# Turning layer-norm rows by DMA transposes of 16-bit pairs, in a two-layer attention and feed-forward kernel

## The reference

```python
x = x + tanh(g_xattn[0]) * L0_xattn(layernorm(x), ctx, ...)   # norm 0: 32 heads of 128, 8 key/value heads
x = x + tanh(g_ffn[0])   * L0_ffn(layernorm(x), A, B, Wr, br) # norm 1: 8 experts of rank 16, softmax router
x = x + tanh(g_xattn[1]) * L1_xattn(layernorm(x), ctx, ...)   # norm 2: 16 heads of 96, 4 key/value heads
x = x + tanh(g_ffn[1])   * L1_ffn(layernorm(x), ...)          # norm 3: gated feed-forward, width 1792
```

## Time and profile before

| what | value |
|---|---|
| median of three executions | 1203.42 us |
| the profiled execution's own time | 1202.64 us |
| its span in the trace | 1200.8 us |
| mean granted TensorE clock | 0.988 |
| TensorE busy | 1140.5 us (95%) |
| VectorE busy | 854.8 us (71%) |
| ScalarE busy | 826.8 us (69%) |
| GpSimd busy | 342.4 us (29%) |

### The profile page before, as it was taken

The page is one execution under the profiler, slowest core; times in us unless marked ns, Lnnn a source line. Parts: engine busy times, 40 slices in busy tenths (PEclk is TensorE's granted clock), DMA queues, the critical chain, the costliest instruction groups (busy, mean ns, idle before and its releaser), DMA issues.

```text
span 1200.8 us, 22840 instructions
## 1 busy us (share of the span) xinstructions
PE 1140.5 (95%) x7264; PEld 721.9 (60%) x7264; DVE 854.8 (71%) x2086; ACT 826.8 (69%) x2699; POOL 342.4 (29%) x644
## 2 busy tenths in 40 slices
PE   6789999999999999999999978899999999799998
PEld 4445666665666666666666555566776766355555
DVE  4578767776777677677677778898888888843434
ACT  5688878888888888888778745578777766522221
POOL 5444333335633333343333421111211121000000
PEclk9899999999999999999999989999999999999999
DMA  7454555554765546545564433467987585300000
GB/s 244 103 115 106 128 140 99 119 139 83 153 115 127 129 103 127 119 103 127 136 107 119 93 58 88 90 99 161 227 200 155 129 170 126 62 2 1 36 1 35
DMA packets 390871, 134.31 MB, mean 112 GB/s; under 512 B 365536, under 2 KB 375520, under 8 KB 390752
## 3 DMA queue, kind: packets, MB, share of 16 engines
q1 hardware_dynamic: 388848, 129.19, 49.2%
q0 software_dynamic: 1904, 3.67, 1.0%
HBM read 39.21 MB, written 2.10 MB: 34 GB/s over the span
## 4 chain that ended last, share of the span: by engine, by line
PE 80%; DVE 9%; ACT 5%; issue 3%; POOL 3%; DMA 0%; DVEq 0%; POOLq 0%; ACTq 0%
PE bank L477 23%; PE bank L479 22%; PE bank L478 22%; PE bank L686 8%; PE bank L705 4%; ACT probs L862 1%; DVE stats L1052 1%; DVE pieces L1041 1%; POOL rstd L1437 1%; DVE mx L1142 1%; PE bank L506 1%; ACT pieces L774 1%; DVE x L1177 1%; ACT junk L777 1%; ACT xT_hi L774 1%
## 5 line engine op out<-in xcount | busy, mean ns | idle before, releaser
L1142 DVE TENSOR_REDUCE mx<-bank 128x2 f32<-128x512 f32 x192 | 131.6, 685 | 56.7 <-PE bank L479 56.6
L774 ACT ACTIVATE pieces<-probs,rs 128x256 f16<-128x256 f32 x384 | 165.2, 525 | 9.1 <-DVE rs L1157 9.0
L862 ACT ACTIVATE probs<-bank,nb,rq 128x256 f32<-128x256 f32 x256 | 141.2, 563 | 40.0 <-DVE nb L1147 39.5
L1041 DVE SCALAR_TENSOR_TENSOR pieces<-probs,rs,pieces 128x256 f16<-128x256 f32 x384 | 163.1, 486 | 4.9 <-ACT pieces L774 4.7
L477 PE MATMUL bank<-wq,xT_hi 128*128 128x512 f16 (+1 forms) x384 | 140.2, 365 | 2.7 <-DVE wq L1041 2.7
L777 ACT ACTIVATE junk<-bank 128x128 bf16<-128x128 f32 x384 | 101.9, 287 | 55.1 <-PE bank L479 55.0
L478 PE MATMUL bank<-wq,xT_hi 128*128 128x512 f16 (+1 forms) x384 | 139.8, 364 | 0.0
L479 PE MATMUL bank<-wq,xT_lo 128*128 128x512 f16 (+1 forms) x384 | 139.8, 364 | 0.0
L477 PE MATMUL bank<-wo_hi,oT 128*128 128x512 f16 x352 | 133.4, 379 | 3.5 <-DVE oT L1041 2.0
L479 PE MATMUL bank<-wo_hi,oT 128*128 128x512 f16 x352 | 133.4, 379 | 0.0
L478 PE MATMUL bank<-wo_lo,oT 128*128 128x512 f16 x352 | 133.4, 379 | 0.0
(11 more groups left out here) (183 smaller groups left out, 2774.5 us busy)
## 6 DMA issues: line engine op xcount, KB each, us to landing
raw_o<-in_wo_a SPq DMA_DIRECT2D x8, 1024.0 KB, 5.8
raw_q<-in_wq_a SPq DMA_DIRECT2D x7, 1024.0 KB, 6.0
raw_kv<-in_wkv_a SPq DMA_DIRECT2D x8, 512.0 KB, 3.8
turned<-pieces SPq DMA_TRANSPOSE x192, 2.8
raw_q<-in_wq_c SPq DMA_DIRECT2D x4, 768.0 KB, 5.0
raw_o<-in_wo_c SPq DMA_DIRECT2D x4, 768.0 KB, 5.6
down_rest<-in_down_t POOLq DMA_DIRECT2D x5, 512.0 KB, 4.2
ff_in<-in_gate_t SPq DMA_DIRECT2D x4, 448.0 KB, 3.8
```

The costliest lines, as they stand in the source:

```text
L774: return act.activation(out, in_, ACT.Copy, scale=scale)
L862: act.activation(probs[:, h, :], bank[h // 2][:, (h % 2) * KV:(h % 2 + 1) * KV], ACT.Exp, bias=nb[:, h:h + 1], scale=scale, accum_out=sums ...
L1041: return dve.scalar_tensor_tensor(out, in_, scale, hi, ALU.mult, ALU.subtract)
L1142: dve.tensor_reduce(mx[:, pr], chunks(bank[i][:, :], 2), AX.X, ALU.max, negate=True).then_inc(mx_done, 1)
```

## The change

Norms 1 and 2, and tiles 4 to 7 of norm 0, no longer go over TensorE and PSUM. The scaled rows `xn` are split where they lie, with tokens on the partitions: the high piece to the left half and the low piece to the right half of a buffer of 1024 16-bit columns (`n_rows`, in the room of `hidden`, which is used at the end only). One DMA transpose from SP then moves its eight 128x128 blocks into both `xT` pieces of that tile, which now lie in one array. For norms 1 and 2 ScalarE makes the high piece (`norm_row_hi`) and GpSimd the low one (`norm_rows`); for norm 0 GpSimd makes both. Readers wait for the transfer (`moved`) in place of `lo`. VectorE's `norm_low`, ScalarE's `norm_hi` and TensorE's `norm_turn` go away for these 20 tiles.

```diff
+def turned_by_dma(k, t):
+    return k in (1, 2) or k == 0 and t >= ROWS0          # ROWS0 = 4
+        def norm_ready(engine, k, t):
+            if turned_by_dma(k, t):
+                engine.wait_ge(norm[k].moved, 16 * (rows_before(k, t) + 1))
+            else:
+                engine.wait_ge(norm[k].lo, t + 1)
...
 # SP
+            def turn_norm(k, t):
+                sp.wait_ge(norm[k].row_lo, rows_before(k, t) + 1)
+                sp.dma_start_transpose(xT_all[:, :, t * P:(t + 1) * P], rows_slot(k)).then_inc(norm[k].moved, 16)
             def step(n):
                 if n - 1 >= N0:
                     move_o(n - 1)
+                if norm0 is not None:
+                    turn_norm(0, norm0)
+                if norm2 is not None:
+                    turn_norm(2, norm2)
+                if norm1 is not None:
+                    turn_norm(1, norm1)
                 if T < N:
                     turn_k(T)
...
 # TensorE, step
                 if lora is not None:
                     lora_project(lora)
-                if norm1 is not None:
-                    norm_turn(1, norm1)
                 if S < N:
                     scores(S)
                 if T < N:
                     q_proj(T)
-                if norm0 is not None:
-                    norm_turn(0, norm0)
-                if norm2 is not None:
-                    norm_turn(2, norm2)
...
 # ScalarE
+            def norm_row_hi(k, t):
+                act.wait_ge(norm[k].xn, t + 1)
+                if t >= 1:
+                    act.wait_ge(norm[k].moved, 16 * t)
+                copy(rows_slot(k)[:, 0:D], xn[xn_slot(k, t)]).then_inc(norm[k].row_hi, 1)
...
                 if T < N:
                     v_hi(T)
+                if norm2 is not None:
+                    norm_row_hi(2, norm2)
                 if norm1 is not None:
-                    norm_hi(1, norm1)
+                    norm_row_hi(1, norm1)
                 if lora is not None:
                     router_exp(lora)
...
-                if norm0 is not None:
-                    norm_hi(0, norm0)
-                if norm2 is not None:
-                    norm_hi(2, norm2)
...
 # VectorE, step
                     router_logits(lora)
-                if norm1 is not None:
-                    norm_low(1, norm1)
...
-                if norm0 is not None:
-                    norm_low(0, norm0)
-                if norm2 is not None:
-                    norm_low(2, norm2)
...
 # GpSimd
+            def norm_rows(k, t):
+                rows, before = rows_slot(k), rows_before(k, t)
+                pool.wait_ge(norm[k].xn, t + 1)
+                if before >= 1:
+                    pool.wait_ge(norm[k].moved, 16 * before)
+                if k == 0:
+                    pool.tensor_copy(rows[:, 0:D], xn[xn_slot(k, t)]).then_inc(norm[k].row_hi, 1)
+                pool.wait_ge(norm[k].row_hi, before + 1)
+                pool.tensor_tensor(rows[:, D:2 * D], xn[xn_slot(k, t)], rows[:, 0:D], ALU.subtract
+                                   ).then_inc(norm[k].row_lo, 1)
...
                     norm_rstd(3, norm3)
+                if norm0 is not None:
+                    norm_rows(0, norm0)
+                if norm2 is not None:
+                    norm_rows(2, norm2)
+                if norm1 is not None:
+                    norm_rows(1, norm1)
                 if T < N0:
                     k_norm(T)
```

More of the change, by code:

```diff
@@ L79, in projected @@
     return n - 2 if n - 2 >= N0 else None
+ROWS0 = 4
 SETS = ((0, 1), (1, 3), (3, NT))
@@ L105, in __init__ @@
         self.xn = sem("xn")
-        self.turned = sem("turned")
-        self.hi = sem("hi")
-        self.lo = sem("lo")
+        if k in (0, 3):
+            self.turned = sem("turned")
+            self.hi = sem("hi")
+            self.lo = sem("lo")
+        if k < 3:
+            self.row_hi = sem("row_hi")
+            self.row_lo = sem("row_lo")
+            self.moved = sem("moved")
 def build(nc, a):
@@ L132, in sb_at @@
             return sb(name, n, dt)
-        xT = tuple(chunks(w, KC) for w in pair("xT", KC * TOK))
+        xT_all = chunks(sb("xT", 2 * KC * TOK, F16)[:, :], 2 * KC)
+        xT = xT_all[:, 0:KC, :], xT_all[:, KC:2 * KC, :]
         cT = tuple(chunks(w, KC) for w in pair("cT", KC * TOK))
@@ L178, in build @@
         hT = [tuple(sb(f"hT{i}_{w}", D, F32R)[:, :] for w in ("hi", "lo")) for i in range(2)]
+        rows_at = [(nc.sbuf_base + 31) // 32 * 32 + i * 4 * D for i in range(2)]
         hidden = [sb(f"hidden{i}", D)[:, :] for i in range(2)]
+        n_rows = [nc.alloc_sbuf_tensor_at(f"n_rows{i}", [P, 2 * D], F16, offset=at)[:, :] for i, at in enumerate(rows_at)]
         down_first = chunks(sb("down_first", 4 * D, F32R)[:, :], 4)
@@ L253, in build @@
         lw_scaled, lw_done, tg_lora_done = sem("lw_scaled"), sem("lw_done"), sem("tg_lora_done")
-        norm = [NormSems(lambda what, k=k: sem(f"norm{k}_{what}")) for k in range(4)]
+        norm = [NormSems(lambda what, k=k: sem(f"norm{k}_{what}"), k) for k in range(4)]
         kv_done, q_done, s_done, pv_done, y_done = (sem(f"{n}_done") for n in ("kv", "q", "s", "pv", "y"))
@@ L413, in step @@
                 S, T = n + 1, n + 3
+                norm0, norm1, lora, norm2, norm3 = beside(n)
                 if n - 1 >= N0:
                     move_o(n - 1)
+                if norm0 is not None:
[4 more added lines that the diff above has]
+                    turn_norm(1, norm1)
                 if T < N:
@@ L494, in norm_turn @@
                     pe.wait_ge(norm[0].lo, t)
[L495 to L498, removed]
                 if k == 3 and 1 <= t < NT - 2:
@@ L517, in kv_proj @@
                 for i in sources:
-                    if n < NT:
-                        pe.wait_ge((ctx_lo, norm[0].lo)[i], t + 1)
+                    if n < NT and i == 0:
+                        pe.wait_ge(ctx_lo, t + 1)
+                    if n < NT and i == 1:
+                        norm_ready(pe, 0, t)
                     if i == 1 and N0 <= n < N0 + NT:
-                        pe.wait_ge(norm[2].lo, t + 1)
+                        norm_ready(pe, 2, t)
                     out = kv_bank(n)[:, i * L.kvw:(i + 1) * L.kvw]
@@ L536, in q_proj @@
                 if n < NT:
-                    pe.wait_ge(norm[0].lo, t + 1)
+                    norm_ready(pe, 0, t)
                 if N0 <= n < N0 + NT:
-                    pe.wait_ge(norm[2].lo, t + 1)
+                    norm_ready(pe, 2, t)
                 for k in range(KC):
@@ L618, in lora_project @@
             def lora_project(t):
-                pe.wait_ge(norm[1].lo, t + 1)
+                norm_ready(pe, 1, t)
                 pe.wait_ge(lw_done, 3)
@@ L1058, in norm_scale @@
                 if k in (1, 2) and t >= 1:
-                    dve.wait_ge(norm[k].turned, t)
-                if k in (0, 3) and t >= 2:
+                    dve.wait_ge(norm[k].row_lo, rows_before(k, t))
+                if k in (0, 3) and t >= 2 and turned_by_dma(k, t - 2):
+                    dve.wait_ge(norm[k].row_lo, rows_before(k, t - 2) + 1)
+                if k in (0, 3) and t >= 2 and not turned_by_dma(k, t - 2):
                     dve.wait_ge(norm[k].turned, t - 1)
```

6 lines of the change are left out of this document (5 added, 1 removed).

## The result

The changed kernel takes 1194.73 us in the median of five executions (1194.38 to 1195.86), the kernel before 1203.17 (1200.07 to 1204.31) in the same session. The ratio is 0.9937, with a 95% interval of 0.9922 to 0.9951: 8.4 us faster by the medians and 7.6 by the ratio, where 16.5 were forecast. The direction is right, the time lies inside the range of 1180 to 1197 and outside the forecast's own 1183 to 1191. The profiled execution took 1195.74 us with a span of 1193.9; the span before was 1200.8, so the two traces show 6.9 us of the gain.

What follows compares the result with a forecast made beforehand. VectorE's list was taken to set the pace in the middle stage. Its terms summed to 13.5 us, with 3.0 early 16.5 us off the profiled 1202.64: 1186.1, given as 1187 us for the median, range 1180 to 1197.

Steps and rivals of the forecast that it cites:

- (e): Middle stage, GpSimd: the 16 subtractions have room; `k_norm` queued behind them makes VectorE wait in step 60, cost 0.8 us.
- middle stage: Step 58's first key/value matmul to step 68's, from 665.18 to 804.31 us: 139.1 us before, about 125.5 us forecast.
- The early stage's term: Steps 0 to 3, norm 0: VectorE loses four `norm_low`, TensorE's waits for `oT` and `xT_lo` shrink; 3.0 us gained.
- (a): Middle stage: `norm_low` leaves VectorE, 15 x 0.60 = 9.0 us, plus about 0.4 us of TensorE transposes for the last tile.
- (b): Middle stage: VectorE's waits before norm 1's `norm_low` go, 6.7 us in 8 waits.
- (c): Middle stage: VectorE's waits for a late TensorE go, 1.4 us before `q_rows` and 0.6 before the row maximum, together 2.0.
- (d): Middle stage, ScalarE: two row copies ahead of the exps delay them 0.3 us in each of six steps, cost 1.8 us.
- (f): Middle stage, TensorE's clock: idle time gathers before `lora_turn`, 2 to 3 us a step; slow stretches behind it cost 2.0 us.
- the clock rival: TensorE slow through `project`, `values` and `lora_project_out` in most steps: 6 to 15 us in place of 2, 1191 to 1200; chance 0.14.
- (g): Middle stage, DMA transposes: eight blocks land in 2.8 us, with 3.5 us of cover in the worst place, cost 0.
- The late-transfer rival: Steps 59 to 67: transfers land late, a loss from 8.4 us of landing, about 1220 us at 10.5; chance 0.06.
- the estimate of 10.5 us: Landing of one eight-block transfer at the Trainium skill's 1309 ns per DMA transpose, one behind the other; would make the change a loss.

Runs made afterwards that it cites:

- e2: Changed kernel with GpSimd's subtraction split into four instructions of 128 columns, nothing left out: 1184.5 us, ratio 0.9857 to the kernel before.
- e1: Changed kernel with GpSimd subtracting only 16 of the 512 columns, so most of the low part is left out: 1181.7 us, ratio 0.9837.
- e7: Changed kernel with 24 filler transposes of the identity on TensorE ahead of the turn of `lora_act`: 1192.0 us, ratio 0.9916.
- e10: Changed kernel with the subtraction in four parts and 16 filler transposes ahead of the turn of `lora_act`: 1185.6 us, ratio 0.9859.
- e12: Changed kernel with four-part subtraction, `k_norm` ahead of norm 1's rows on GpSimd, and 16 filler transposes ahead of the turn of `lora_act`: 1185.2 us, ratio 0.9856.
- e8: Changed kernel with four-part subtraction and `k_norm` ahead of norm 1's rows on GpSimd in steps 58 to 60: 1186.4 us, ratio 0.9862.
- e11: Changed kernel with four-part subtraction and the row maxima in an unused PSUM bank: 1185.1 us, ratio 0.9855.
- e3: Changed kernel with eight filler transposes of the identity on TensorE ahead of the turn of `lora_act`: 1193.6 us, ratio 0.9936.
- e4: Changed kernel with the low pieces of norms 1 and 2 formed by VectorE instead of GpSimd, ahead of the row maximum: 1202.3 us, ratio 1.0012.
- e5: Changed kernel with norm 0 turned by TensorE and split by ScalarE and VectorE as before the change: 1196.8 us, ratio 0.9949.
- e6: Changed kernel with GpSimd's subtraction split into two instructions of 256 columns: 1189.1 us, ratio 0.9887.

## Why the prediction was only half right, step by step

**The step that failed** is in (e), where the prediction said that the 16 subtractions "have room" on GpSimd and counted only what is queued behind them there. The room was there: GpSimd is busy for 52.08 of 140 us. Missing was a term for what a GpSimd instruction does to VectorE's: 9.0 us of hold in the middle stage, all on the list that sets the pace. The stage takes 6.5 us more than forecast (132.0 for 125.5), and with the hold cut to some 2 us and nothing else changed (e2) it takes 124.4, 1.1 less than forecast. The early stage's term of 3.0 us came out at 1.5, with holds of 0.93 us on one `nb` and 1.25 on the `wo_lo`; in e2 the same way, from `xn` of tile 3, is 2.9 us shorter than before. The span of e2 is 17.5 us below the span before, where 16.5 were forecast for the whole. The sum that was worked out is nearly that of a kernel whose GpSimd instructions are short. That it fits so closely is in part luck: e2 still has 2 us of hold, waits 2.9 us for `kr` where 0.8 were priced, and pays less than priced for ScalarE and for the clock.

The trace before could have shown it. Behind the middle stage, where keys are split on GpSimd all the time, `sums_in` runs into such a split, VectorE and then GpSimd:

```profile
811.25 0.45 DVE L1155 TENSOR_SCALAR sums_in<-sums 128x4 f32<-128x4 f32 x1 [0.61 <-ACT probs L862]
811.73 0.18 DVE L1157 RECIPROCAL rs<-sums_in 128x4 f32<-128x4 f32 x1
```

```profile
811.13 0.55 POOL L1463 TENSOR_TENSOR k_rows<-kn,k_rows 128x192 f16<-128x192 f32 x1
```

`sums_in` takes 0.45 us in place of 0.17 and ends at 811.70, GpSimd's instruction at 811.68.

The Trainium skill has this rule. Its page "SBUF — State Buffer", section "Who interferes with whom", says that VectorE's second pair of SBUF ports is GpSimd's only one, that it is taken for a whole instruction, and that the other engine "fully blocks"; it names as takers on VectorE's side instructions with two SBUF inputs and those in a 2-port mode, which it gives to `tensor_scalar` and denies to `tensor_reduce`. The traces agree: `nb` as TENSOR_TENSOR and as TENSOR_SCALAR, and `lg`, are held to the end of the subtraction, `mx` and every form with its stream in PSUM are not. The prediction weighed the page on transposes, whose price the trace had already answered, and not this one.

(a), (b), (c) The work and the waits went as stated. No `xT_lo` stands in the stage, the 6.7 us of the earlier trace rows and the 1.4 before `q_rows` are gone, and the scores start right behind the experts' projection. A turn of VectorE is 14.5 and 15.05 us in the changed kernel (724.32 to 738.86 to 753.91) and not the 13 forecast; with the hold gone, in e1, it is 13.2 (706.17 to 719.41). By TensorE's side the early stage was read wrongly: the wait of `project` for `oT` that stood at 96.30 did not shrink, it is 1.70 us in place of 0.70, which fits a TensorE that comes to it sooner while VectorE sets the pace.

(d) ScalarE's copies did not delay the exps in the changed kernel, since these waited for the held `nb`: VectorE waits 0.9 us in 2 for them, which is less than the 1.1 before. With the hold gone (e1) they wait 1.3 us in 4 within the stage, of which 0.3 us fall in two of the steps with two norms, against 1.1 in 2 before. Forecast were 1.8 us more, 0.3 in each of six such steps: the place is right and the size too high.

(e) As to what is queued on GpSimd: 0.4 us in 1 for `kr`, forecast 0.8. In e2, with 1.7 us of GpSimd a tile, it is 2.9 in 2.

(f) The clock term had the right place and a size that hangs on something else. The idle time before the turn is 19.1 us in 7, up to 3.4 where I said 2 to 3, `project` is slow in three steps, and e7 puts the price at 2.9 us for a forecast of 2. In e1, e10 and e12 no `project` is slow, in e2 one is and in e8 and e11 two are, and the times of e2, e8, e11 and e12 cannot be told from e10's: without the long hold, the term is too small to measure. So the clock rival was not what happened, though it named a time (1191 to 1200 us) that holds the result.

(g) The transfers of 8 blocks into rows 2 KB apart land in 2.8 us in the median (2.7 to 4.6), as the earlier trace rows said. TensorE waited for them 1.4 us in 2, in the early stage alone; in the other traces it is 0.8 to 4.1 us there, so "no wait" held in the middle stage (but for 0.2 us in e1) and not in the early one. The late-transfer rival is out, and with it the estimate of 10.5 us from the price of one transpose.

From 810 us on all was to be as before. From step 68 to the end the trace before takes 396.5 us and the changed kernel's 398.2; the twelve others take 396.7 (e2) to 399.6 (e3), half of them over 397.6. Ten of the thirteen traces with the change have one or two waits of 0.9 to 1.3 us for transfers of probabilities there, where the one trace before has none. That is a term of about 1 us which the prediction put at nothing; its cause stays open.

## What to carry to other kernels

Work that is moved to an idle engine is not free because that engine has room: ask what it does to the engine that sets the pace, and look in the trace for small instructions of the busy engine that begin while a long one of the other runs. When VectorE sets the pace, keep GpSimd's instructions short: four of 0.43 us held VectorE's `nb` for 1.1 us where one of 1.16 us held it for 9.0, although GpSimd worked 25.1 us in place of 18.2. An experiment with the suspected instruction cut nearly to nothing, and one with it split, tell a hold from a shared rate in two runs.

## What the runs showed of the hardware that I had not expected

- A VectorE instruction that begins beside a GpSimd one can be held to that one's end. A 128x2 instruction of 0.16 us took up to 1.09 us, one of 0.23 up to 1.05. The other way round, the subtraction took up to 1.73 us for 1.15 in the early stage, beside VectorE's instructions with two SBUF inputs.
- The hold takes TENSOR_TENSOR with both inputs in SBUF and TENSOR_SCALAR from SBUF to SBUF, at 2, 4 and 8 elements a partition. GpSimd's CAST holds too: in e1 `sums_in` at 736.55 us takes 0.36 instead of 0.17 and ends at 736.91, where a CAST of `k_rows` ends at 736.88. RECIPROCAL from SBUF to SBUF (0.15 us) and everything with its stream in PSUM went free beside the same subtraction.
- GpSimd's subtraction took 0.22 us for 16 columns, 0.43 for 128, 0.67 for 256 and 1.15 for 512: about 0.2 us fixed and 1.9 ns a column, so by an estimate from these four sixteen parts would take some 4 us.
- A long hold on VectorE can cost twice: once itself, and again through TensorE's clock. TensorE idled for 19.1 us before the turn with the hold and for 13.4 without (e1), and behind such idle times stood `project` groups of 4.1 to 4.4 us in place of 2.75, in e4, e5 and e6 also of 5.3. Filling the idle time with the hold in place (e7) made the stage 2.9 us shorter.
